# First attention's scores: fp32 queries and keys, two heads on two halves of the array's rows, and new instruction orders

## What is computed

```python
x = x + tanh(g_xattn[0]) * L0_xattn(ctx, layernorm(x))    # 8 heads of 64, keys: 77 context + 512 own tokens
x = x + tanh(g_ffn[0])   * L0_ffn(layernorm(x))           # 8-bit rounded FFN with a depthwise convolution
x = x + tanh(g_xattn[1]) * L1_xattn(layernorm(x), ctx)    # 16 heads of 8, rotary, keys: 77 context tokens
x = x + tanh(g_ffn[1])   * L1_ffn(layernorm(x))           # 8 experts, top 2, and a shared expert
```

```python
q = q / scale                                  # scale = 64 ** -0.5
sim = einsum('bhid,bhjd->bhij', q, k)          # 512 queries x 589 keys, contraction over 64
attn = softmax(sim, axis=-1)
out = einsum('bhij,bhjd->bhid', attn, v) @ Wout
```

## Time and profile before

| | before |
|---|---|
| median of 3 runs | 267.66 us (267.06 to 267.77) |
| the profiled execution's own time | 267.53 us |
| its span, first to last instruction | 265.7 us |
| TensorE busy | 254.0 us (96%), 1847 matmuls |
| VectorE busy | 218.1 us (82%), 534 instructions |
| ScalarE busy | 193.1 us (73%), 463 instructions |
| mean granted TensorE clock | 0.986 |

### The profile page before, as it was taken

How to read it: one execution, slowest core, us unless ns; L and a number is a source line. 1 busy time by engine, 2 the same in 40 slices (tenths; PEclk the granted TensorE clock), 3 DMA queues, 4 the chain that set the end, 5 groups by cost and what they waited for, 6 DMA issues and landing times.

```text
span 265.7 us, 5563 instructions
## 1 busy us (share of the span) xinstructions
PE 254.0 (96%) x1847; PEld 189.1 (71%) x1847; DVE 218.1 (82%) x534; ACT 193.1 (73%) x463; POOL 31.1 (12%) x53
## 2 busy tenths in 40 slices
PE   7899999999999999999999999959999999999996
PEld 3567779779778878768788787747756565565675
DVE  6499979866766698998999887888999999899861
ACT  1589887788658678688899965268999689834551
POOL 3000002000000011101100102200003110424130
PEclk9999999999999999999999999977999999999999
DMA  6183391300400004300300000000000000000001
GB/s 190 32 242 104 90 331 42 90 4 0 93 1 1 2 17 98 69 0 6 88 4 0 0 2 0 4 0 1 2 0 4 1 4 0 2 0 10 23 10 39
DMA packets 8848, 10.70 MB, mean 40 GB/s; under 512 B 1115, under 2 KB 5877, under 8 KB 8821
## 3 DMA queue, kind: packets, MB, share of 16 engines
q1 hardware_dynamic: 7792, 9.70, 13.6%
q10 hardware_dynamic: 1029, 0.65, 0.8%
HBM read 4.99 MB, written 0.52 MB: 21 GB/s over the span
## 4 chain that ended last, share of the span: by engine, by line
PE 68%; DVE 17%; issue 7%; ACT 6%; POOL 1%; DVEq 0%; ACTq 0%; POOLq 0%
PE slot L516 19%; PE slot L605 12%; PE slot L586 6%; PE slot L587 6%; PE slot L561 3%; PE slot L754 2%; DVE mx L1145 2%; PE slot L567 2%; ACT S L903 2%; PE slot L748 2%; PE slot L612 2%; DVE RB L1150 2%; PE slot L699 2%; PE slot L742 2%; PE slot L576 2%
## 5 line engine op out<-in xcount | busy, mean ns | idle before, releaser
L1039 DVE TENSOR_REDUCE nm<-slot 128x1 f32<-128x589 f32 x64 | 47.6, 765 | 9.7 <-PE slot L587 9.3
L831 ACT ACTIVATE PR<-slot,nm 128x589 f32<-128x589 f32 x64 | 47.8, 750 | 9.3 <-DVE nm L1039 8.7
L516 PE MATMUL slot<-K,PR 128*128 128x128 f32 (+1 forms) x320 | 44.3, 276 | 0.2
L586 PE MATMUL slot<-KH,Q 128*128 128x296 f32 (+1 forms) x128 | 42.1, 345 | 0.2
L516 PEld LDWEIGHTS slot<-K,PR 128*128 128x128 f32 (+1 forms) x320 | 36.0, 142 | 8.2 <-ACT PR L831 5.0
L605 PE MATMUL slot<-PT,V 128*64 128x256 f32 (+1 forms) x320 | 38.1, 384 | 0.7 <-ACT PT L766 0.7
L766 ACT ACTIVATE PT<-slot 128x640 f32<-128x640 f32 x47 | 32.2, 706 | 8.3 <-PE slot L516 7.3
L587 PE MATMUL slot<-KL,Q 128*128 128x296 f32 (+1 forms) x128 | 36.1, 299 | 0.0
L903 ACT ACTIVATE S<-slot,mx 128x77 f32<-128x77 f32 x128 | 29.4, 371 | 6.2 <-DVE mx L1145 5.6
L605 PEld LDWEIGHTS slot<-PT,V 128*64 128x64 f32 (+1 forms) x320 | 22.1, 137 | 12.3 <-issue 3.5
L586 PEld LDWEIGHTS slot<-KH,Q 128*128 128x128 f32 x128 | 24.2, 189 | 3.6 <-issue 1.4
(11 more groups left out here) (169 smaller groups left out, 478.9 us busy)
## 6 DMA issues: line engine op xcount, KB each, us to landing
KH<-KH SPq DMA_DIRECT2D x16, 147.5 KB, 2.5
KL<-KL SPq DMA_DIRECT2D x16, 147.5 KB, 2.6
CTT<-in_ctxT SPq DMA_DIRECT2D x1, 640.0 KB, 3.9
K<-in_const SPq DMA_DIRECT2D x1, 589.0 KB, 5.0
WGU<-in_wgu SPq DMA_DIRECT2D x1, 580.0 KB, 6.3
out<-X SPq DMA_DIRECT2D x8, 64.0 KB, 1.5
L1W<-in_l1w SPq DMA_DIRECT2D x1, 384.0 KB, 3.7
WD<-in_wdT SPq DMA_DIRECT2D x1, 320.0 KB, 6.8
```

Source lines behind the costliest of these rows:

```text
L516: return pe.transpose(dst, src, ident[0:p, 0:p])
L586: pe.matmul(W[:, K0 + lo:K0 + hi], q, KH[:, g % 4, lo:hi], start=True, stop=False)
L831: act.activation(PR[:, s, :], W[:, K0:K0 + KEYS0], ACT.Exp, bias=nm0[:, s:s + 1], accum_out=sum0[:, b, p * 2 + f, t, e:e + 1]).then_inc(pr ...
L1039: dve.tensor_reduce(nm0[:, s:s + 1], W[:, K0:K0 + KEYS0], AX.X, ALU.max, negate=True).then_inc(max_ready, 1)
```

## The change

Queries and keys are stored whole, in fp32, as `Q` and `KT`, each in four buffers (`HOMES`), one for each pair of heads: one copy by ScalarE of 128 rows each, no subtraction, no doubling by DMA. The two heads' score tiles are formed together when the second head's front comes up. For each column half there are two matmuls, one on rows 0 to 63 and one on rows 64 to 127, into different banks. Each tile's last matmul raises a semaphore of its own, `scores_ready`. Values get a buffer for each batch, and the second batch's copies of them no longer wait for the first batch's last value product. The string `PLAN` is new throughout.

```diff
@@ -102,46 +103,45 @@
-x0:F6 x0:A1 k:F0 q:F6 k:A1 k:F2 k:D1 q:A1 v:F4 q:D1 v:F0 k:A1 v:Ca k:D1 u:F6 u:F2 v:Ca u:F4 u:D1 u:D1 u:A1 u:A1 u:F0 u:D1
+x0:F2 x0:A1 k:F4 k:A1 v:F0 q:F2 q:A1 u:F2 v:Cd k:F4 u:F6 u:D1 k:A1 u:F4 u:A1 u:F0 u:D1 u:B u:A1 u:B u:D1 u:A1 u:D1 u:Ca
...
+a4:A1 o:D1 a4:F0 o:D1 a4:B a1:P1 a4:D1 a4:Ca n:P2 n:D3 a4:F4+12@6 a4:B f1:F7 a4:D1 a2:F6 a4:A1 a4:Ca a4:B f1:A1 f1:D1 f2:F2 a2:D1 a4:Ca f2:F0
...
-        Q = sb("Q", [P, 2, 2, S], F32R)
-        KH = sb("KH", [P, 4, KEVEN], F32R)
-        KL = sb("KL", [P, 4, KEVEN], F32R)
-        V = sb("V", [P, 5, IN0])
+        Q = sb("Q", [P, HOMES, S])
+        KT = sb("KT", [P, HOMES, KEVEN])
+        V = sb("V", [P, B, 5, IN0])
...
-            def double(g):
-
-                for e in range(2):
-                    r, o = slice(e * DH0, (e + 1) * DH0), slice((1 - e) * DH0, (2 - e) * DH0)
-                    s = (2 * g + e) % 4
-                    for part, signal in ((KH, k_upper), (KL, k_ready)):
-                        sp.wait_ge(signal, 2 * g + e + 1)
-                        sp.dma_start(part[o, s, :].bitcast(F32), part[r, s, :].bitcast(F32)).then_inc(k_doubled[g % 2][e], 16)
-
-            double(0)
...
+                if kind == "u":
+                    if item[5] == 1:
+                        scores(item)
+                    return
...
+            def scores(item):
+
+                _, b, p, f, t, _ = item
+                g = b * NP0 + p
+                pe.wait_ge(q_ready, g + 1)
+                pe.wait_ge(k_ready, g + 1)
+                for lo, hi in ((0, KA), (KA, KEVEN)):
+                    for e in range(2):
+                        rows = slice(e * DH0, (e + 1) * DH0)
+                        mm = pe.matmul(slot(("u", b, p, f, t, e))[:, K0 + lo:K0 + hi],
+                                       Q[rows, g % HOMES, (f * TP + t) * P:(f * TP + t + 1) * P], KT[rows, g % HOMES, lo:hi],
+                                       start=True, stop=True)
+                        if lo:
+                            mm.then_inc(scores_ready, 1)
...
-            if b == 1:
-                engine.wait_ge(front_done, NTH["w", 0, NP0 - 1, 1] + 1)
...
+                    if g >= HOMES:
+                        act.wait_ge(scores_ready, 8 * (g - HOMES + 1))
+                    act.activation(Q[:, g % HOMES, :], W[:, 0:S], ACT.Copy, scale=float(DH0) ** 0.5).then_inc(q_ready, 1)
...
+                    act.activation(KT[:, g % HOMES, :], W[:, K0:K0 + KEVEN], ACT.Copy).then_inc(k_ready, 1)
...
-                if kind == "q":
-                    for e in range(2):
-                        dve.wait_ge(q_upper, 2 * n - 1 + e)
-                        r, o = slice(e * DH0, (e + 1) * DH0), slice((1 - e) * DH0, (2 - e) * DH0)
-                        s = (n - 1) % 2
-                        dve.scalar_tensor_tensor(out=Q[o, s, e, :], in0=W[r, 0:S], scalar=float(DH0) ** 0.5,
-                                                 in1=Q[r, s, e, :].bitcast(F32), op0=ALU.mult,
-                                                 op1=ALU.subtract).then_inc(q_ready, 1)
```

More of the change, by code:

```diff
@@ L44 @@
 BANKS = 8
+HOMES = 4
 RING = 3
@@ L176 @@
 ORDER, BANK_OF, HAD, COPIES, WARM = orders()
-NTH = {x: n for n, x in enumerate(x for x, stage in ORDER["PE"] if stage == "F")}
+NTH = {x: n for n, x in enumerate(x for x, stage in ORDER["PE"] if stage == "F" and x[0] != "u")}
 def copied(item, engine):
@@ L303, in mega_kernel @@
         v_copied = {"ACT": sem("v_by_act"), "DVE": sem("v_by_dve")}
-        q_upper = sem("q_upper")
         q_ready = sem("q_ready")
-        k_upper = sem("k_upper")
         k_ready = sem("k_ready")
-        k_doubled = [[sem(f"k_doubled{i}{e}") for e in range(2)] for i in range(2)]
+        scores_ready = sem("scores_ready")
         max_ready = sem("max_ready")
@@ L438, in _ @@
             sp.dma_start(BO[:], bo.broadcast_to([P, D])).then_inc(ld["l1"], 16)
-            double(2)
+            sp.wait_ge(k_ready, 2)
             wo = wout.rearrange("(p e r) d -> e r p d", e=2, r=P)
@@ L447, in _ @@
             sp.dma_start(WD[:], wdT.rearrange("(c p) d -> p c d", p=P)).then_inc(ld["moe"], 16)
-            for g in range(3, B * NP0):
-                double(g)
             ov = out.rearrange("(t p) d -> t p d", p=P)
@@ L578, in front @@
                     mm = pe.matmul(W[:, 512:K0 + KEVEN], WK[:, p, :], LT[:, b, KA:KEVEN], start=True, stop=True)
-                elif kind == "u":
-                    _, b, p, f, t, e = item
-                    g = b * H0 + 2 * p + e
-                    pe.wait_ge(q_ready, 2 * (g // 2 + 1))
-                    pe.wait_ge(k_doubled[g // 2 % 2][e], 32 * (g // 4 + 1))
-                    q = Q[:, g // 2 % 2, e, (f * TP + t) * P:(f * TP + t + 1) * P]
-                    for lo, hi in ((0, KA), (KA, KEVEN)):
-                        pe.matmul(W[:, K0 + lo:K0 + hi], q, KH[:, g % 4, lo:hi], start=True, stop=False)
-                        mm = pe.matmul(W[:, K0 + lo:K0 + hi], q, KL[:, g % 4, lo:hi], start=False, stop=True)
                 elif kind == "w":
@@ L604, in front @@
                             h = 2 * p + e
-                            mm = pe.matmul(W[e * DH0:(e + 1) * DH0, 0:N], V[0:r, c, h * DH0:(h + 1) * DH0],
+                            mm = pe.matmul(W[e * DH0:(e + 1) * DH0, 0:N], V[0:r, b, c, h * DH0:(h + 1) * DH0],
                                            PT[0:r, s, c, e, :], start=(c == 0), stop=(c == 4))
@@ L787, in copy_values @@
             engine.wait_ge(front_done, NTH[item] + 1)
-            if b == 1:
-                engine.wait_ge(front_done, NTH["w", 0, NP0 - 1, 1] + 1)
             rows, n = (P, 2) if j < 2 else (C, 1)
-            dst = V[0:rows, 2 * j:2 * j + n, :].rearrange("p c d -> p (c d)")
+            dst = V[0:rows, b, 2 * j:2 * j + n, :].rearrange("p c d -> p (c d)")
             if by == "ACT":
@@ L1019, in first @@
                 W, n = slot(item), upto(item)
[L1020 to L1035 removed]
+                if kind == "u":
+                    dve.wait_ge(scores_ready, n)
+                else:
+                    dve.wait_ge(front_done, NTH[item] + 1)
+                if kind == "u":
                     s = (n - 1) % RING
```

93 lines of the change are left out of this document (37 added, 56 removed).

## The result

The changed kernel takes 305.0 us (median of four runs, 301.2 to 305.9) against 267.5 us. The ratio is 1.132 [1.126, 1.139], which is 302.8 us. The profiled execution took 304.11 us for a span of 302.3 us. The forecast was 269.6 us and the range ended at 273.6, so the direction that had the most weight was right and the size was missed by some 33 us.

The account below looks back on a forecast made before the run. The prediction took TensorE's matmuls to bound the attention phase. Its terms, 4.9 + 1.5 - 3.1 + 1.2 - 2.6 = +1.9 us, added to the median of 267.66 us, gave 269.6 us, with a range of 264.4 to 273.6 us.

Parts of the forecast that it names:

- Part 1: Attention scores on TensorE: a lone pair of heads, fp32 side by side, costs 1.29 us for 1.10; +4.9 us.
- Rivals B: Attention scores: the two heads of a pair do not run side by side; +31.7 us, 301 us, chance 0.05.
- C: Attention scores: weight loads of a pair are exposed; 9.6 us more, 279 us, chance 0.07.
- Part 2: Attention phase: dropping the splitting lightens VectorE and ScalarE, giving back half of TensorE's 6.1 us waits; -3.1 us.
- Part 3: Start of the kernel: the new order makes TensorE wait between the first pairs and transposes; +1.5 us, bounds 0 and 2.5.
- Parts 4 and 5: Change of stage: work moved ahead of last value product, +1.2 us; tail: faster TensorE and earlier exponentials, -2.6 us.
- Part 4: Change of stage: a query projection and score tile move ahead of the last value product, five warm-ups go; +1.2 us.
- A: Attention phase and tail: freed engines end TensorE's waits, 6.1 us back and 4.0 from the tail; 265.2 us, chance 0.35.
- D: Tail: transposes do not hold the clock, so 1.8 us stay lost; 271.4 us, chance 0.11.

Follow-up runs that it names:

- run 5: Changed kernel with only its table rewritten for the first attention (order, slots, copiers), scores still in pairs: 280.8 us, ratio 1.052.
- run 6: Changed kernel with simplified scores at the old cost, tiles issued singly, and a table rewritten for them: 267.2 us, ratio 0.999.
- run 11: Changed kernel with its table rewritten a second time, starting from the changed kernel's own order, scores in pairs: 278.1 us, ratio 1.043.
- runs 5 and 9: The first as in its own line, 280.8 us; the second has its order with simplified scores at the old cost, issued in pairs: 277.1 us.
- runs 12 to 14: Kernel before, attention table rewritten twice: 269.1 and 270.0 us; last, its own attention phase with the changed kernel's order afterwards: 268.2 us, ratio 1.005.
- run 3: Changed kernel's order, buffers and copies, with simplified scores at the old cost, each tile issued singly: 298.6 us, ratio 1.115.

## Why the prediction was wrong, step by step

**Part 1 (scores, +4.9 us): right.** A pair takes 1.19 us, the heads run side by side, and the price is 4.3 us in the changed kernel's order and 3.8 us in run 5's, a little under the forecast. Rivals B (a pair near 2.1 us) and C (near 1.5 us) are refuted by the same rows. The Trainium skill, "TensorE: Matmul & The Clock Gate", Part 3, says in one place that weight loads overlap matmuls in flight only when their row groups differ, and in another that a load into the background weight buffer may also go ahead. The trace of a pair doesn't agree with the first: eight loads, four of them to each half, leave 1.19 us for eight passes.

**Part 2 (the splitting goes, -3.1 us): this step failed**, and with it the range. It took the waits of the earlier trace rows as a stock of 6.1 us from which the change could only take, "0 the lower one". In the same sentence stood that "a pair now needs two wide PSUM slots at once", and it was given no price. The new order of the middle of the phase got none either. The busy times of the two engines fell about as worked out, and run 6 shows what that is worth: 1.4 us at most, and nothing against the kernel before. Against it stand 27 us of new idle time on TensorE. Their source is not the joint issue as such, for pairs and singles run alike in one and the same order (298.8 and 298.6; 277.1 and 277.4). It is the table: with the code unchanged a new one takes back 21 to 24 us. With four wide slots and three buffers `PR`, a round of a pair's scores (1.19 us), a maximum (0.77), an exponential (0.75), transposes (0.55) and a copy (0.70) takes 4.0 us for the first tile alone. As I read the traces, the kernel is only full where other tiles stand in between on every engine, and where no list holds a ready tile behind a wait. The old table kept TensorE's idle time at 1.1 us. The new one has neither, and I had read from it only what moved at the two ends.

By ratios: the changed kernel 302.8 us; with another table 279.0 (run 11), so 23.8 us were the table, with about 1 us of it the lower clock; scores at the old cost 3.8 less (runs 5 and 9), some 275 us; single tiles with their own order 267.2 (run 6), so some 8 us between the best tables for pairs and for single tiles, probably for keeping a pair's tiles together; the kernel before 267.4. The range's high end was mis-added too: its terms give 274.0, not 273.6. Both are far below the result.

**Part 3 (the start, +1.5 us): its walk came out right, in part by luck.** The third pair starts at 20.42 us (I said 20.6), and the fourth tile's transposes end at 22.22 us (I said 22.4), when a chunk pair of values is still to come:

```profile
14.35 2.26 PE L697 MATMUL slot<-KT,Q 64*128 64x296 f32 x16
17.34 2.23 PE L500 MATMUL slot<-K,PR 128*128 128x128 f32 x15 [0.74 <-ACT PR L823]
...
20.42 1.26 PE L697 MATMUL slot<-KT,Q 64*128 64x296 f32 x8 [0.84 <-DVE PT L762]
21.61 0.77 PE L500 MATMUL slot<-K,PR 128*128 128x128 f32 x5
22.22 1.88 PE L549 MATMUL slot<-WV,LT 128*128 128x512 f32 x4
```

On the way two errors offset each other. The first keys begin at 8.63 us and not at 9.24, and TensorE then waits 0.7 us for ScalarE's copy of the queries, which my walk left out. The scores of the first pair are there for VectorE at 15.64 us (I said 15.3). The price of 1.5 us itself was measured by no run.

This was the one place where I walked all the lists. Done for the whole phase, the same walk might have shown the waits.

**Parts 4 and 5 (change of stage and tail, -1.4 us together): wrong in sign.** The tail of the changed kernel is 3.8 us shorter than that of before cut at the same place, more than the 2.6 forecast. But the last of runs 12 to 14 puts both parts together at 1.2 us slower (0.6 to 1.8, from its interval). Part 4 counted two of the steps that were moved ahead of the last value product (1.7 us); TensorE's work in the phase rose by 2.6 us and its idle time by 1.5.

**The rivals.** A is out: TensorE's waits grew. D is out too. In the changed tail the clock is full where the FFN's matmuls run, and so it is in the kernel of before with that tail (0.99 over the tail, 0.96 before, where it fell to 0.50):

```profile
216.00:222.00 6.00, 5.81 (x38) 4.21 (x36) 5.41 (x10) 5.14 (x12) 0.00 (x0) 1.00 0.00 0
```

The Trainium skill, same page, Part 4, says that transposes don't count as TensorE being busy in the same way; here a tail whose wait is filled with transposes kept its clock. Whether the transposes held it, or the other matmuls that stand closer together there (the 2.6 us wait is gone), no run separates. The case that came true, an order that doesn't fit its tiles, was none of my rivals.

## What to carry to other kernels

Where an order is written by hand for engines that walk their lists, a change of the work and a change of the order are two changes: compare each alone, and the new work under an order made for it. When a profile shows the bounding engine without idle time, its few waits say what one order achieves, not what the next one will; a new order must be walked through on all engines over the whole phase, not only where it moves things at the ends. Busy time taken off engines that the bounding one hardly waits for is worth little, however much it is: here 15 us less of VectorE gave 0 to 1.4 us.

## What the hardware showed beside this

**The clock falls inside the attention phase.** The changed kernel has two stretches at the lower level, 1.2 GHz (the columns are those of the stages above; TensorE's granted clock is the last but two):

```profile
64.20:69.20 5.00, 3.40 (x28) 2.67 (x28) 2.74 (x13) 1.44 (x3) 0.00 (x0) 1.00 0.01 3
69.30:72.60 3.30, 3.30 (x18) 3.30 (x17) 1.95 (x8) 1.57 (x4) 0.40 (x1) 0.50 0.00 0
132.40:137.40 5.00, 2.96 (x21) 2.05 (x18) 3.29 (x5) 2.79 (x5) 1.06 (x2) 1.00 0.00 0
137.60:140.80 3.20, 3.20 (x12) 1.47 (x10) 0.30 (x1) 0.78 (x1) 0.00 (x0) 0.50 0.00 0
```

TensorE had been busy 3.40 and 2.96 of 5.0 us before the two falls. In the profiled executions of the kernel before and of runs 5 and 11 the clock never falls in this phase. At half the clock the two stretches are worth up to 1.6 us each, half of 3.3 and of 3.2. The executions bear this out: the changed kernel took 304.11 us at a mean granted clock of 0.987 and 301.23 at 0.999, and run 3 took 299.6 at 0.989 and 297.4 to 297.6 at 1.00. So waits may cost twice. They don't always: from 118 to 123 us TensorE is busy 3.08 of 5.0 us, and the clock stays full. What brings a fall about is not shown.

**Two fp32 heads on two row halves.** Four fp32 matmuls of 294 to 296 columns, two for each half, take 1.19 us from the first load to the next whole-array load. Four single passes for each of two tiles over the whole array take 1.10 us (8 x 0.137). Going in costs some 0.1 us more: the passes before the pair at 59.16 start at 58.57 and 58.82, and the next would be due at 59.06. Over the 32 pairs the runs put the price at 3.8 and 4.3 us, so 0.12 to 0.13 us a pair, when the halves run side by side.
